# Taking the norm behind the last attention apart: three batches between that attention's last steps, the fourth at its end

## The reference

```
x = x + LN(L0_attn(LN(x)))
x = x + LN(L0_ffn(LN(x)))      # attention, then 16 experts, 4 chosen
x = x + LN(L1_attn(LN(x)))     # "the last attention": 16 heads of 16
x = x + LN(L1_ffn(LN(x)))      # 16 experts, 4 chosen, and 2 shared ones
```

## Time and profile before

| | us |
|---|---|
| median of 3 runs | 2736.82 (2732.43 to 2748.43) |
| the profiled execution, its own time | 2739.3 |
| its span, first to last instruction | 2737.5 |
| busy in the span: PE / DVE / ACT / POOL | 2346.8 / 1612.9 / 1301.6 / 1305.3 |
| mean granted TensorE clock | 0.930 |

### The profile page before, as it was taken

One profiled execution on the slowest core, in us unless ns is written; L12 is line 12 of the kernel. 1 busy time (PEld: TensorE's weight loads), 2 busy tenths in 40 slices (PEclk: granted clock), 3 DMA queues, 4 the chain that ended last, 5 costly groups with the idle time before them and its releaser, 6 DMA issues. The chain is left out here.

```text
span 2737.5 us, 40991 instructions
## 1 busy us (share of the span) xinstructions
PE 2346.8 (86%) x12100; PEld 1564.8 (57%) x12100; DVE 1612.9 (59%) x5239; ACT 1301.6 (48%) x3694; POOL 1305.3 (48%) x1309
## 2 busy tenths in 40 slices
PE   5999999995899999999999599982578787699992
PEld 5888888883355555555555456551233343567661
DVE  5767676764666766766775533335566654553334
ACT  4444444444456656656666334432166566343332
POOL 2544454440455555555555168870644220038883
PEclk8999999997999999999999689995789999699996
DMA  5000000002000000000000635552000000515555
GB/s 170 1 16 15 15 15 15 16 5 89 1 1 1 1 1 1 1 1 1 2 1 1 252 65 86 86 79 85 0 1 1 1 1 0 201 32 87 85 87 120
DMA packets 72818, 112.26 MB, mean 41 GB/s; under 512 B 11504, under 2 KB 59632, under 8 KB 72240
## 3 DMA queue, kind: packets, MB, share of 16 engines
q0 software_dynamic: 30336, 42.73, 9.9%
q1 hardware_dynamic: 42304, 67.34, 7.2%
HBM read 80.69 MB, written 36.32 MB: 43 GB/s over the span
## 5 line engine op out<-in xcount | busy, mean ns | idle before, releaser
L1064 POOL TENSOR_TENSOR b_sm<-b_sm,b_rden 128x128 f32<-128x128 f32 (+3 forms) x512 | 355.1, 720 | 355.4 <-DVE b_rden L1017 355.3
L957 ACT ACTIVATE b_sm<-b_sm,b_mn 128x128 f32<-128x128 f32 (+3 forms) x512 | 284.8, 568 | 22.9 <-DVE b_mn L1009 21.6
L948 ACT ACTIVATE b_pt<-b_t 128x128 f32<-128x128 f32 (+3 forms) x512 | 195.2, 438 | 143.1 <-PE b_t L888 143.0
L1009 DVE CUSTOM_DVE_ANT_0 b_sm<-b_f,maskB 128x128 f32<-128x128 f32 (+3 forms) x512 | 233.6, 489 | 2.8 <-issue 1.6
L878 PE MATMUL b_f<-b_k,b_q 64*128 64x128 f32 (+3 forms) x1024 | 209.5, 485 | 28.9 <-DVE b_prod L998 14.5
L998 DVE SCALAR_TENSOR_TENSOR b_prod<-b_f,b_sin 32x512 f32<-32x512 f32 x320 | 219.8, 687 | 4.3
L2085 DVE TENSOR_REDUCE c_nm<-c_first 128x2 f32<-128x1024 f32 x128 | 155.0, 1219 | 85.2 <-PE c_first L1840 85.2
L1433 POOL DMA_INDIRECT XN<-rows,m_slots x158 | 157.6, 998 | 94.0 <-issue 47.2
L1985 ACT ACTIVATE c_pt<-c_second 128x512 f32<-128x512 f32 x256 | 139.2, 598 | 123.4 <-PE c_second L1853 123.1
L888 PE MATMUL b_t<-ident,b_sm 128*128 128x128 f32 x1280 | 193.3, 281 | 1.1 <-ACT b_pt L948 0.8
L888 PEld LDWEIGHTS b_t<-ident,b_sm 128*128 128x128 f32 x1280 | 142.3, 141 | 87.5 <-issue 60.3
(11 more groups left out here) (290 smaller groups left out, 5341.6 us busy)
## 6 DMA issues: line engine op xcount, KB each, us to landing
WM<-in_m_w_dram SPq DMA_DIRECT2D x4, 3072.0 KB, 17.2
WM<-in_m_w_dram SPq DMA_DIRECT2D x4, 2432.0 KB, 13.9
acc<-in_zeros_dram SPq DMA_DIRECT2D x3, 2176.0 KB, 15.4
n_part<-acc SPq DMA_DIRECT2D x12, 512.0 KB, 7.5
a_wa<-in_a_wa_dram SPq DMA_DIRECT2D x8, 512.0 KB, 4.4
b_w<-in_b_w_dram SPq DMA_DIRECT2D x1, 3072.0 KB, 10.1
XN<-rows,m_slots POOLq DMA_INDIRECT x158, 2.8
X<-in_x_dram SPq DMA_DIRECT2D x4, 512.0 KB, 5.7
```

Source lines behind the costliest of these rows:

```text
L948: act.activation(pt[:, M % 2, head, 0:t + 1, t * P:(t + 1) * P], back_bank(("t", S, head))[:, 0:keys(t)].rearrange("p (k n) -> p k n", n=P ...
L957: act.activation(sm[:, s, 0:keys(t)], sm[:, s, 0:keys(t)], ACT.Exp, scale=-1.0, bias=mn[:, s:s + 1], accum_out=den[:, s:s + 1]).then_inc(s ...
L1009: dve.tensor_tensor_reduce(sm[:, s, 0:keys(t)], front_bank(("s", S, head))[:, 0:keys(t)], mask[:, SEQ - keys(t):SEQ], 1.0, -3 * NEG, ALU.a ...
L1064: pool.tensor_tensor(sm[:, s, 0:keys(t)], sm[:, s, 0:keys(t)], rden[:, s:s + 1].to_broadcast([P, keys(t)]), ALU.mult).then_inc(s_pn, 1)
```

## The change

The block "n4" is gone. Its work for the first three batches is put into steps of `attention2`, its work for the fourth stands behind the last step:

- DVE takes the statistics of Y of batches 0, 1 and 2 in steps 124, 125 and 126, the sums into X from step 129, the statistics of X from step 130. ACT takes the two square roots, each for three batches at once, in steps 128 and 134, and the normed rows in steps 143, 145 and 147; they now go to Y, not XN.
- PE turns the normed rows in steps 145 to 150 and makes the router's product in steps 147, 149 and 151. Both go through the bank p_x and stand in its list `singles`; each half batch of a turn is copied by ACT alone (`copy_turned`), each batch of logits by DVE (`copy_logits`).
- The same is done for batch 3 after the loop, one thing after the other. The loop ends two steps earlier; these had nothing in them.
- The statistics of Y and of X share one buffer, and ACT writes its square roots over norm_of_x.
- SP stores the rows from within the attention. The loads of `ws`, the constants, `before` and all four groups of expert weights are issued when the block of experts starts. Only the router's weights are loaded earlier, with the attention's own.

The diff, cut to what the prediction speaks of:

```diff
@@ moe
+        lg = c.lgs if shared else sb("lg", [P, TILES, EXPERTS])
...
             @block.sync
             def _(sp):
-                for g in range(GROUPS // 2, GROUPS):
+                for dst, src, done in c.first_loads:
+                    sp.dma_start(dst, src).then_inc(done, 16)
+                for g in range(0 if shared else GROUPS // 2, GROUPS):
                     fetch(sp, g)
@@ attention2
-    FIRST_STEP, LAST_STEP = -PER_BATCH, NP - PER_BATCH + 62
+    FIRST_STEP, LAST_STEP = -PER_BATCH, NP - PER_BATCH + 60
+    STATS, ROOT_Y, SUM, ROOT_X, NORM, TURN_X, LOGITS = NP - 4, NP, NP + 1, NP + 6, NP + 15, NP + 17, NP + 19
+    EARLY = BATCH - 1
...
+        for k in range(KD):
+            if early_at(s, TURN_X + k, 2) is not None:
+                singles.append(("h", early_at(s, TURN_X + k, 2) * KD + k))
+        if early_at(s, LOGITS, 2) is not None:
+            singles.append(("lg", early_at(s, LOGITS, 2)))
+    singles += [("h", EARLY * KD), ("h", EARLY * KD + 1), ("lg", EARLY)]
...
+                def turn_x(n):
+                    b, k = n // KD, n % KD
+                    pe.wait_ge(s_xn, b + 1)
+                    single_free(("h", n))
+                    for t in tiles(b):
+                        x = pe.transpose(p_x[:, t % TB * P:(t % TB + 1) * P], c.Y[:, t, k * P:(k + 1) * P], c.ident[:, :])
+                    x.then_inc(s_tx, 1)
+
+                def logits(b):
+                    pe.wait_ge(s_ht, (b + 1) * KD)
...
+                    single_free(("lg", b))
+                    for t in tiles(b):
+                        for k in range(KD):
+                            x = pe.matmul(p_x[:, t % TB * EXPERTS:(t % TB + 1) * EXPERTS], c.HT[:, k, t * P:(t + 1) * P], c.gw[:, k, :],
+                                          start=(k == 0), stop=(k == KD - 1))
+                    x.then_inc(s_lg, 1)
...
+                for k in range(KD):
+                    turn_x(EARLY * KD + k)
+                logits(EARLY)
...
+                    if s == ROOT_Y:
+                        root_y(0, EARLY)
+                    if s == ROOT_X:
+                        root_x(0, EARLY)
+                    if early_at(s, NORM, 2) is not None:
+                        normalise(early_at(s, NORM, 2))
+                    for k in range(KD):
+                        if early_at(s, TURN_X + k, 2) is not None:
+                            copy_turned(early_at(s, TURN_X + k, 2) * KD + k)
+                root_y(EARLY, 1)
+                root_x(EARLY, 1)
+                normalise(EARLY)
+                for k in range(KD):
+                    copy_turned(EARLY * KD + k)
...
+                    if early_at(s, STATS, 1) is not None:
+                        stats_y(early_at(s, STATS, 1))
+                    if s == SUM:
+                        inverse_y(0, EARLY)
+                    if early_at(s, SUM, 1) is not None:
+                        sum_x(early_at(s, SUM, 1))
+                    if early_at(s, SUM + 1, 1) is not None:
+                        stats_x(early_at(s, SUM + 1, 1))
+                    if s == ROOT_X + 1:
+                        inverse_x(0, EARLY)
+                    if early_at(s, LOGITS, 2) is not None:
+                        copy_logits(early_at(s, LOGITS, 2))
@@ sandwich
-            norm_stage(nc, c, "n4", outs=((c.HT, None, None),), fetch=fetch1, store=rows0, gate=m1_gate,
-                       prefetch=((c.cst[:, :], m_const, c.s_cst), (c.ws[:, :, :], m1_shared, c.s_ws),
-                                 (c.before[:, :, :], before.to_broadcast([P, EXPERTS, EXPERTS]), c.s_before)))
+                c.first_loads = ((c.ws[:, :, :], m1_shared, c.s_ws), (c.cst[:, :], m_const, c.s_cst),
+                                 (c.before[:, :, :], before.to_broadcast([P, EXPERTS, EXPERTS]), c.s_before))
```

More of the change, by code:

```diff
@@ L1168, in moe @@
         EARLY = (TILES * DIM - 2 * NBC * EXPERTS) // RCOLS
-        bank = [c.p_lg] + [st.enter_context(nc.psum_tensor(f"{name}_p{i}", [P, SEQ], F32)) for i in range(1, 8)]
+        bank = [] if shared else [c.p_lg]
+        bank += [st.enter_context(nc.psum_tensor(f"{name}_p{i}", [P, SEQ], F32)) for i in range(len(bank), 8)]
         p_x, p_h, p_a, p_y = bank[0:2], bank[2:4], bank[4:6], bank[6:8]
@@ L1636, in own @@
                             product(j)
-                logits_in()
+                if not shared:
+                    logits_in()
                 own(0)
@@ L1671, with attention2 @@
 C_PAIRS = C_HEADS // 2
-def attention2(nc, c):
+def attention2(nc, c, store):
     NH = 2 * C_HEADS
@@ L1703, in batch_at, with early_at @@
         return (s - after) // PER_BATCH if (s - after) % PER_BATCH == 0 and 0 <= (s - after) // PER_BATCH < BATCH else None
+    STATS, ROOT_Y, SUM, ROOT_X, NORM, TURN_X, LOGITS = NP - 4, NP, NP + 1, NP + 6, NP + 15, NP + 17, NP + 19
+    EARLY = BATCH - 1
+    def early_at(s, first, apart):
+        b = (s - first) // apart
+        return b if (s - first) % apart == 0 and 0 <= b < EARLY else None
     KEYS_AT, PROJ_AT, V_AT, O_AT, A_AT, OUT_AT = 23, 0, 16, 29, 55, 58
@@ L1785, in attention2, with _ @@
         with nc.Block() as block:
+            @block.sync
+            def _(sp):
+                for b in range(BATCH):
+                    sp.wait_ge(s_xn, b + 1)
+                    sp.dma_start(store[b * SEQ:(b + 1) * SEQ, 0:DIM].rearrange("(t p) d -> p t d", p=P), of(c.Y, b)).then_inc(c.s_stored, 16)
             @block.tensor
@@ L1993, in copy_a, with root_y, root_x, normalise @@
                     act.activation(a_f[:, k, :], p_x[:, :], ACT.Copy).then_inc(s_af, 1)
+                def root_y(first, n):
+                    act.wait_ge(s_mvy, first + n)
+                    at = slice(first * TB, (first + n) * TB)
+                    act.activation(sdy[:, at], mvy[:, at, 1], ACT.Sqrt, bias=c.eps[:, :]).then_inc(s_sdy, 1)
+                def root_x(first, n):
+                    act.wait_ge(s_mvx, first + n)
+                    at = slice(first * TB, (first + n) * TB)
+                    act.activation(sdy[:, at], mvy[:, at, 1], ACT.Sqrt, bias=c.eps[:, :]).then_inc(s_sdx, 1)
+                def normalise(b):
+                    act.wait_ge(s_offx, 1 if b < EARLY else 2)
+                    for t in tiles(b):
+                        x = act.activation(c.Y[:, t, :], c.X[:, t, :], ACT.Identity, bias=offy[:, t:t + 1], scale=rsy[:, t:t + 1])
+                    x.then_inc(s_xn, 1)
+                def copy_turned(n):
+                    b, k = n // KD, n % KD
+                    act.wait_ge(s_tx, n + 1)
+                    act.activation(c.HT[:, k, b * SEQ:(b + 1) * SEQ], p_x[:, :], ACT.Copy).then_inc(s_ht, 1)
                 act.wait_ge(s_w, 128)
@@ L2324, in sandwich @@
                        prefetch=((c.cst[:, :], m_const, c.s_cst),))
+            c.first_loads = ()
             moe(nc, c, "m0", M0_HIDDEN, rows0, acc0, fetch, s_wm, ff_ln_w, False)
             c.free_semaphores()
[L2327 to L2340 removed]
```

139 lines of the change are left out of this document (104 added, 35 removed).

## The result

The changed kernel takes 2761.29 us, median of 6 runs (2759.69 to 2767.04), against 2738.46 of the kernel before in the same session. The ratio is 1.0079, 95% interval [1.0065, 1.0094]: slower, by 18 to 26 us. Forecast were 2754 and a range of 2738 to 2766. The profiled execution took 2762.08 us, its span is 2760.3.

The account below looks back on a forecast made before the run. It took these stretches as bound by chains of latencies, no engine full before routing. Terms 4.2 + 4.5 + 18.4 + 5 - 23.3 + 8.1 = +16.9 on 2739.3 gave 2756.2; 2.5 lower for the median, 2753.7, said 2754; range 2738 to 2766 us.

Parts of the forecast that it names:

- Statistics of Y in steps 124 to 126: Late attention: three batches' statistics on DVE ahead of maxima that PE's scores wait for; +4.2 us, bounds 0 and 5.2.
- Two roots: Between ACT's exponentials: two roots, each with two table loads, 2.26 us each; +4.5 us, at most 4.8 by another row.
- The sums hidden, with 2 us to spare: DVE after the last maximum: 10.5 us of sums, statistics of X and offsets cost nothing, with 2 us to spare.
- Insertions in the tail: Last exponential to output: three normed rows, six turns, three router products inserted; +18.4 us, bounds 9.1 and 21.0.
- its clock: Attention's tail: insertions at half clock, which they don't raise; +5 us, bounds 0 and 12.5.
- "n4" goes: Block "n4" off, 40.7 us; batch 3's norm on, 17.4 us in a chain; -23.3 us, at full clock -25.9.
- Loads: Experts' start: silu 0 waits for the constants on ACT, 10.8 us after the start; +8.1, lower bound 7.3 (`ws` alone), upper 10.
- Clock holds: Rival: the clock stays up in the tail and the loads come well; +8.5 us, 2745; chance 0.33.
- Moved work hidden: Rival: moved work slips into idle time of DVE, ACT and POOL; -15.2 us, 2722; chance 0.07 hidden or half hidden.
- Table loads that hold ACT longer: Rival: each of the four table loads holds ACT another 1.28 us, exponentials end 5.1 us later; 2759; chance 0.04.
- Root waiting for DVE: Rival: step 134's root waits 2 or 3 us for DVE, delaying fourteen exponentials; 2756; chance 0.56 together with the forecast.

Follow-up runs that it names:

- no_roots: Changed kernel with DVE making the inverse roots of batches 0 to 2, no ACT table loads there; ratio 1.0057 to the kernel before.
- all_in_time: all_parts with the third sum and two statistics of X behind DVE's copy of the heads' output, two Newton steps for three; ratio 0.9925 to the kernel before.
- late_loads: Kernel before with only the loads of shared experts' weights, constants, `before` and expert weights issued at the experts' start; ratio 1.0013 to the kernel before.
- all_parts: late_products plus statistics of Y in steps 128 to 130, inverse roots on DVE, `ws`, constants and `before` loaded mid-attention; ratio 0.9925 to the kernel before.
- other_banks: Changed kernel with turns in the scores' four banks, router products in the transposed scores' two, two engines copying; ratio 1.0013 to the kernel before.
- late_products: other_banks with the router products of batches 0 to 2 moved behind the last output product; ratio 0.9980 to the kernel before.

## Why the prediction was right, and where not

*Statistics of Y in steps 124 to 126*, +4.2: 4.6, and taking them away gave 4.6 back. Right, with the reason: three statistics ahead of the maxima, for which DVE had 0.4 us of idle time.

*Two roots*, +4.5: 5.9 in the profile after, 6.8 when they were taken out. The mechanism was right and the term mis-sized, in the step that counted 2.26 us each. The 2.93 us between the exponentials are as forecast; what was left out is that PE stands still meanwhile and goes on at 1.2 GHz, with pairs of exponentials 1.97 or 2.60 us apart instead of 1.68. I had put 3 us for this stretch only into the upper bound of the clock's term. The rows of PE after the change show where its clock fell:

```profile
2307.30 0.79 PE L1894 MATMUL c_second<-c_qt,c_kt 64*128 64x512 f32 x2 [4.63 <-ACT c_pt L2053]
...
2325.60 0.50 PE L1894 MATMUL c_second<-c_qt,c_kt 64*128 64x512 f32 x2 [2.51 <-ACT c_pt L2053]
...
2327.27 0.80 PE L1894 MATMUL c_second<-c_qt,c_kt 64*128 64x512 f32 x2 [1.17 <-ACT c_pt L2053]
```

Only the second fall stands behind a root. The first follows the wait for the late maxima, when the first root had not begun to hold PE up, and no_roots has it too (0.79 us at 2307.87, behind 4.59 us of waiting). So the statistics cost more than the 4.6 us of their own stretch; by estimate some 0.9 more, the difference between no_roots (25.47) and all_in_time (24.55), whose maxima are not held up and whose clock stays at 1.00. The size of the roots' term is uncertain by some 2 us: the same code of before took 26.40 us here in one profile, at a clock of 0.87, and 24.57 in late_loads.

*The sums hidden, with 2 us to spare*: right. The second root's table load has no wait before it (DVE had the statistics at 2319.2, the load starts at 2321.55). How thin this is showed in all_parts, where DVE was busy for 22.24 us of this stretch, not 13.09, and its copy of the heads' output came late.

*Insertions in the tail*, +18.4, *and its clock*, +5: together 24.9. The runs split the sum by mechanism: 13.3 by the bank p_x and the single copying engine (other_banks), 10.0 by three products (late_products), 1.6 left. The products and turns were priced at full clock, and of the 7.9 us for half clock I took 5. In the tail all three products (3.56 us each, 1.82 at full clock) and four of the six turns (1.09 us, not 0.63) ran at half clock, which is 7.1 us by these rows; the rest of the sum was a little too dear, and the two misses partly cancel. No run gives the clock's share by itself.

*"n4" goes*, -23.3: 23.0. The chain of single rows was the best term of all, because in this block nothing overlaps with anything.

*Loads*, +8.1: 6.4 in the profile after, 5.7 alone, 6.4 when moved forward. Wrong was the landing: `ws` took 6.3 us, not the 7.3 of the earlier trace rows, and the constants, issued 0.4 us behind it and not 2.1, let ACT go on at 7.0 instead of 9.0. Wrong with it was the path: the sum went by the constants on ACT, but silu 0 waited last for PE, so `ws` alone set the +6.4, as in the lower bound. In the five other versions that issue `ws` first in the experts' block behind the changed attention it took 6.4 to 6.8 us. The row that I took stood in a queue with other loads; whether that made it 7.3 no run shows. The Trainium skill ("DMA: Bandwidth & Descriptors", Anatomy of one DMA) fits its formula to DMAs that GpSimd issues; taken for this one, which SP issues, it gives 4.9 us by estimate. All twelve traces are above it, with 5.5 to 7.3.

*What I did not forecast*: 4.6 us ahead of step 124, where the change adds nothing. I take it for chance: over the twelve profiles, in which the code up to there does the same steps in the same order (four of them with the early loads beside it), the maximum of step 124 starts between 2287.0 and 2298.1, and the kernel before alone took from 2732.5 to 2750.1 us in its 32 runs of one session. From 2160 to 2200 the clock is 1.00 in the profile of before and 0.91 in that of after:

```profile
2160.00:2200.00 40.00, 31.75 (x184) 14.23 (x184) 30.42 (x44) 23.92 (x43) 15.41 (x16) 1.00 0.00 1
```

```profile
2160.00:2200.00 40.00, 31.90 (x167) 14.27 (x166) 28.96 (x41) 21.47 (x36) 15.70 (x15) 0.91 0.00 1
```

Without it and the last row of the table the profiles differ by 18.7 us, against 16.9 forecast; the ratio of many runs gives 18 to 26.

*The rivals.* Clock holds: wrong, 0.58 in the tail. Moved work hidden: wrong as the change was written; but late_products shows that most of what stood in the tail can be hidden, by six other banks, a second copying engine and another place for three products. The list of the bank, named against this rival, was the largest part. Table loads that hold ACT longer: the root starts 0.01 us behind its load (2307.27 + 1.28, 2308.56); the drain of 1.38 us of the Trainium skill ("ScalarE: Activation LUTs", What ACT_TABLE_LOAD costs) doesn't show. Its advice to do all of one set before switching (Rules for kernel authors) was right all the same: without the four loads and two roots, which last 5.7 us, the stretch was 6.8 us shorter. Root waiting for DVE: did not happen.

## What to carry to other kernels

Work that leaves a block of chains for an engine "with idle time" must be checked against its place in each queue and each buffer's list of users, not against busy shares: 23 us were saved and 35 paid, of which other banks and another order gave 23 back. A wait on one engine can cost more than itself where another engine's clock falls meanwhile (in all_parts ACT waited 3.76 us, and the stretch was 4.7 us longer than in all_in_time), so price a gap with the rows behind it at half clock. And where runs of the same kernel differ by 0.5%, cut the profiles at marks: most stretches whose code was the same agreed to 0.4 us, and the others differed by about 2, where the starts of step 124 moved by 11.

## What the hardware showed that I had not expected

Stretches come in steps rather than in a spread: from silu 0 to the slots it is 54.2 to 54.7 us in ten of the twelve profiles and 56.35 in the other two. The router's product of one batch took 3.56 us at half clock and half of 3.64 at full clock, and PE counts as busy all the time in both. The load of 1216 KB took 7.3 us in the kernel before, 6.3 to 6.8 where it was issued first in the experts' block behind the changed attention, 5.7 there behind the old one, and 5.5 to 5.7 in the middle of the attention.
